# Two attention layers on one core: hand-ordered first and last steps, paired loads, and a second bank for two late outs

## The reference

```python
# layer 0 (layer 1 alike, with its own mask: k = -inf and v = 0 where masked)
xn = layernorm(x) * ln_w + ln_b
q = xn @ Wq + bq
k = xn @ Wk + bk + (1.0 - src_mask) * -1e6
q = softmax(q over the features of a head)
k = softmax(k over the tokens)
v = (xn @ Wv + bv) * src_mask
att = einsum('bnhd,bnhl->bhdl', k, v)
y = einsum('bnhd,bhdl->bnhl', q, att)
scale, shift = split(silu(emb) @ W_emb + b_emb)
h = layernorm(y) * ln2_w + ln2_b
h = h * (1 + scale) + shift
x = x + silu(h) @ W_out + b_out
```

## Time and profile before

| | us |
|---|---|
| median of 3 runs | 306.34 |
| lowest and highest | 303.88 and 311.64 |
| the profiled execution's own time | 306.14 |
| its span, first to last instruction | 304.4 |
| mean granted TensorE clock | 0.947 of full |

### The profile page before, as it was taken

How to read it: one execution, slowest core, us unless ns; L and a number is a source line. 1 busy time by engine, 2 the same in 40 slices (tenths; PEclk the granted TensorE clock), 3 DMA queues, 4 the chain that set the end, 5 groups by cost and what they waited for, 6 DMA issues and landing times.

```text
span 304.4 us, 8956 instructions
## 1 busy us (share of the span) xinstructions
PE 264.1 (87%) x2746; PEld 191.2 (63%) x2746; DVE 261.3 (86%) x870; ACT 215.9 (71%) x497; POOL 222.6 (73%) x296
## 2 busy tenths in 40 slices
PE   1615899779999999998999999999989999987564
PEld 1302576556777777775777677777767776765342
DVE  2791677899999999999999999999998888789851
ACT  1352776678887888877899989999997987663210
POOL 1342336799999999999999989999998776753300
PEclk9955999999999999999999999999999999999755
DMA  7599956874566676796469866565599779753945
GB/s 230 181 264 277 266 66 189 158 100 103 107 100 128 131 148 122 122 129 124 104 99 120 151 92 133 129 123 126 128 137 132 155 147 156 165 132 106 163 103 182
DMA packets 91006, 43.59 MB, mean 143 GB/s; under 512 B 71952, under 2 KB 85072, under 8 KB 90960
## 3 DMA queue, kind: packets, MB, share of 16 engines
q1 hardware_dynamic: 84048, 34.90, 62.5%
q10 hardware_dynamic: 6912, 8.13, 9.2%
HBM read 21.94 MB, written 4.29 MB: 86 GB/s over the span
## 4 chain that ended last, share of the span: by engine, by line
PE 50%; POOL 21%; issue 14%; DMA 6%; DVE 4%; ACT 2%; SPq 1%; ACTq 1%; POOLq 0%; DVEq 0%
PE ps_qv L1262 16%; PE ps_eo L1299 11%; PE ps_k L1242 9%; PE ps_y L1361 5%; POOL h L217 5%; POOL y_z L642 4%; POOL h_half L212 4%; POOL k_mask L630 4%; DMA zt_hi<-z_hi 3%; PE ps_eo L1280 3%; PE ps_eq L1333 2%; PE ps_eq L1314 2%; DMA m1c<-in_mask_col 2%; DMA film_ab<-film_rows 1%; POOL x_rstd L608 1%
## 5 line engine op out<-in xcount | busy, mean ns | idle before, releaser
L478 ACT ACTIVATE v<-ps_qv,v_mask 128x256 f32<-128x256 f32 x64 | 30.2, 472 | 41.8 <-PE ps_qv L1262 41.8
L1262 PE MATMUL ps_qv<-w_hi,zt_hi 128*128 128x512 f16 x128 | 48.7, 381 | 1.7 <-DVE q_sub L920 1.7
L1262 PE MATMUL ps_qv<-w_lo,zt_hi 128*128 128x512 f16 x128 | 48.5, 379 | 0.0
L1262 PE MATMUL ps_qv<-w_hi,zt_lo 128*128 128x512 f16 x128 | 48.5, 379 | 0.0
L642 POOL TENSOR_SCALAR y_z<-y_n,y_rstd,y_shift 128x256 f32<-128x256 f32 x64 | 37.3, 592 | 10.8 <-DVE y_shift L1015 10.8
L1299 PE MATMUL ps_eo<-wo_hi,gt_hi 128*128 128x256 f16 x128 | 37.3, 291 | 7.5 <-DVE x_all L1055 7.5
L1242 PE MATMUL ps_k<-zt_hi,w_hi 128*128 128x256 f16 x128 | 35.4, 276 | 8.3 <-issue 8.3
L673 POOL TENSOR_TENSOR x_all<-x_all,row_b 128x512 f32<-128x512 f32 x32 | 41.0, 1280 | 0.0
L1299 PE MATMUL ps_eo<-wo_hi,gt_lo 128*128 128x256 f16 x128 | 37.2, 291 | 0.0
L1299 PE MATMUL ps_eo<-wo_lo,gt_hi 128*128 128x256 f16 x128 | 37.2, 291 | 0.0
L1361 PEld LDWEIGHTS ps_y<-att_e,eq_t 128*128 128x128 f32 x256 | 33.8, 190 | 5.1 <-issue 1.0
(11 more groups left out here) (98 smaller groups left out, 682.1 us busy)
## 6 DMA issues: line engine op xcount, KB each, us to landing
film_ab<-film_rows SPq DMA_DIRECT2D x32, 256.0 KB, 3.8
m_row<-mask_rows SPq DMA_DIRECT2D x32, 128.0 KB, 3.4
out<-x_all SPq DMA_DIRECT2D x16, 256.0 KB, 2.5
x_all<-in_x ACTq DMA_DIRECT2D x2, 1024.0 KB, 10.8
wemb<-in_w_emb ACTq DMA_DIRECT2D x2, 1024.0 KB, 7.7
x_all<-in_x ACTq DMA_DIRECT2D x1, 1536.0 KB, 13.5
w_raw<-in_w_in SPq DMA_DIRECT2D x1, 768.0 KB, 4.9
w_raw<-in_w_in ACTq DMA_DIRECT2D x1, 768.0 KB, 13.8
```

The costliest lines, as they stand in the source:

```text
L478: nc.scalar.activation(part(v[p], t), ps_qv[:, t * BANK + D:(t + 1) * BANK], ACT.Copy, scale=v_mask[a.layer][:, m:m + 1]).then_inc(v_ready ...
L1262: last = mm(part(ps_qv, t, BANK), zz[p][:, (t * C + c) * P:(t * C + c + 1) * P], w[l][:, c * W + D:(c + 1) * W], start=(n == 0), stop=(n = ...
```

## The change

Every engine gets functions first_steps() and last_steps() beside step(s). The first and last items are called one by one with at(j), in an order of their own, and only the items between go through the loop. The step in the loop has another order too, with small offsets (item(s, 0) to item(s, 18)).

Loads: x comes in pairs of sequences (X_GROUPS: 1, 1 and then seven times 2), the first pair after z_high(0) and no longer before ACT's loop. wemb, wo, w_raw[1] and row_b[1] are issued one at a time at later steps, and wo and wemb have a semaphore each. w_raw[0] is loaded in two parts, k columns and qv columns, after the two small mask rows. What is loaded is the same.

film_scale stays on POOL up to item 29 (SCALE_ON_DVE = 30), film_shift up to item 27 as before. The out products of items 29 and 31 (ASIDE) go to ps_k, which is free after the last k_shift; items 30 and 31 so don't wait for the residual just before them. late_products is defined, and nothing calls it. UNUSED stays 0.

The core of the diff (the lists of first_steps are cut, and the weights' and film operations that hang on a value of s are moved with the rest):

```diff
-    FILM_ON_DVE = LAST - 4
+    SCALE_ON_DVE, SHIFT_ON_DVE = LAST - 2, LAST - 4
+    ASIDE = (LAST - 3, LAST - 1)
+    X_GROUPS = ((0, 1), (1, 1)) + tuple((i, 2) for i in range(2, B, 2))
+        def out_bank(a):
+            return ps_k[:, :] if a.index in ASIDE else ps_eo[:, :]
# SP
             load(col[:, :], columns, col_in)
-            load(w_raw[0][:, :].rearrange("p (c n) -> p c n", c=C), w_in[0].rearrange("(c p) n -> p c n", p=P), w_in_s[0])
             load(m0r[:, :], mask0_row, mask_in)
             load(m1r[:, :], mask1_row, mask_in)
+            load_columns(0, D, wk_in[0])
+            load_columns(D, 2 * D, wqv_in[0])
             def step(s):
...
+                do(film_rows_of, item(s, 10))
+                do(mask_row, item(s, 7))
+                do(store, item(s, 18))
+                do(turn_g_high, item(s, 13))
+                do(turn_g_low, item(s, 13))
+                do(turn_z_high, item(s, 6))
+                do(turn_z_low, item(s, 6))
# ACT
-            load_sequences(2, 4, x_in[2])
                 if s == 0:
-                    load_chunked(wo_raw[0], w_out[0], C, w_late_in[0])
-                    load_chunked(wemb[0], w_emb[0], EC, w_late_in[0])
-                    load_sequences(6, 4, x_in[3])
+                    load_group(2)
                 if s == 1:
-                    load_chunked(w_raw[1], w_in[1], C, w_in_s[1])
-                    load(row_b[1][:, :], rows[1].partition_broadcast(P), rows_in[1])
-                if s == 2:
-                    load_sequences(10, B - 10, x_in[4])
+                    load_chunked(wemb[0], w_emb[0], EC, wemb_in[0])
+                if s == 2:
+                    load_group(3)
+                    load_chunked(wo_raw[0], w_out[0], C, wo_in[0])
+                if s == 3:
+                    load_chunked(w_raw[1], w_in[1], C, wqv_in[1])
+                if s == 4:
+                    load_group(4)
+                    load(row_b[1][:, :], rows[1].partition_broadcast(P), rows_in[1])
+                if 5 <= s < len(X_GROUPS):
+                    load_group(s)
# POOL
+            def step(s):
+                do(k_scaled_heads, item(s, 4))
+                do(x_power, item(s, 1))
+                do(y_power, item(s, 6))
+                do(normalise_y, item(s, 6))
+                do(film_shift, item(s, 7))
+                do(add_out_bias, item(s, 1))
+                do(film_scale, item(s, 6))
+                do(x_variance, item(s, 0))
# DVE
+            def first_steps():
+                fold_columns(0)
+                fold_columns(1)
+                x_statistics(at(0))
+                x_aggregate(at(0))
+                mask_rows()
+                block_masks()
+                x_offset(at(0))
+                x_statistics(at(1))
...
+                z_low(at(0))
+                silu_cond()
+                sum_of_parts()
+                k_weights(0)
+                x_statistics(at(2))
+                k_weights_low(0)
...
+                k_shift(at(0))
+                qv_weights_low(0)
+                value_masks()
+                x_statistics(at(4))
+                x_statistics(at(5))
+                z_low(at(2))
+                q_maximum(at(0))
...
+            def step(s):
+                do(att_scale, item(s, 5))
+                do(y_variance, item(s, 6))
+                do(gate, item(s, 8))
+                do(q_maximum, item(s, 4))
+                do(y_offset, item(s, 6))
+                do(x_offset, item(s, 1))
+                do(residual, item(s, 10))
+                do(q_shift, item(s, 4))
+                do(g_low, item(s, 8))
+                do(k_shift, item(s, 3))
+                do(y_sums, item(s, 5))
+                do(x_statistics, item(s, 0))
+                do(y_divide, item(s, 5))
+                do(x_aggregate, item(s, 0))
+                do(y_statistics, item(s, 5))
+                do(k_sums, item(s, 3))
+                do(y_aggregate, item(s, 5))
+                do(z_low, item(s, 1))
+            def last_steps():
...
+                gate(at(30))
+                film_scale(at(31))
+                g_low(at(30))
+                film_shift(at(31))
+                residual(at(28))
+                gate(at(31))
+                residual(at(29))
+                g_low(at(31))
+                residual(at(30))
+                residual(at(31))
# PE
+            def first_steps():
+                k_weight_rows(0)
+                qv_weight_rows(0)
+                project_k(at(0))
+                unused_products()
+                film_products(0)
+                project_qv(at(0), 0)
+                project_qv(at(0), 1)
+                film_part_sums(0)
+                turn_exp_k(at(0), at(-1))
+                project_k(at(1))
...
+            def step(s):
+                do(project_k, item(s, 3))
+                do(attention_out, item(s, 5))
+                do(turn_exp_k, item(s, 4), item(s, 10))
+                do(project_qv, item(s, 3), 0)
+                do(attend, item(s, 4), item(s, 5))
+                do(project_qv, item(s, 3), 1)
+                do(project_out, item(s, 9), item(s, 4))
+                do(turn_exp_q, item(s, 4), item(s, 4))
+            def last_steps():
...
+                attention_out(at(31))
+                project_out(at(26), at(-1))
+                project_out(at(27), at(-1))
+                project_out(at(28), at(-1))
+                project_out_aside(at(29))
+                project_out(at(30), at(-1))
+                project_out_aside(at(31))
```

596 lines of the change are left out of this document (417 added, 179 removed).

## The result

The changed kernel takes 293.7 us (median of 4 runs, 292.72 to 294.65); the kernel before took 307.68 beside it (303.88 to 311.64). The ratio is 0.9626, with a 95% interval of 0.954 to 0.9711. Executions more than 1.5% above the fastest of their kernel are left out of a ratio but not of a median, so a ratio isn't the quotient of the two medians. The forecast was 294.0. The profiled execution took 292.72 us for a span of 290.9.

What follows compares the result with a forecast made beforehand. No engine alone was the bound: PE, DVE and POOL are full together in layer 0, with idle time at the ends. Start 28.0, middle 230.0 and end 34.1 sum to 292.1, plus 1.7 around the span: 294 us, range 285 to 305.

Steps and rivals of the forecast that it cites:

- The start: Span up to project_k(1): forecast 28.0 us against 34.05, bounds 25 and 32, a gain of 6.0.
- It runs at the half clock as it does now: project_k(0) on PE, starting at 17: half clock, 2.7 us, ending at 19.7.
- The middle: From project_k(1) to project_k(31): forecast 230.0 us against 229.96, no gain, bounds 226 and 239.
- I give that 2 us of the 3.5: z transposes issued together and earlier: 2 us less of PE's 3.5 us idle time from 140 to 265 us.
- 0.2 x 15 = 3.0: Layer 0, POOL waiting for DVE's y_offset between y_power and normalise_y: 0.2 us in 15 steps, 3.0 us more.
- PE's work between the two project_k is nearly the same: Middle, project_k(1) to project_k(31): nearly the same set of products as before, 222 us of PE work.
- The end: From project_k(31) to the end: forecast 34.1 us against 40.4, bounds 31.5 and 38.
- With items 29 and 31 in ps_k, out(31) waits only for its own transpose ... Gain 2.4: End, g_low(31) to finish: no wait for the residual before out(31), 9.4 or 9.5 us against 11.9.
- Ahead of it DVE is full and its order decides: End, before g_low(31): film_scale to POOL 1.2 us, film_ab wait 1.1, other DVE idle time 1.6 gone.
- (b): Rival: start lost, x pairs arrive one by one behind weights, project_k(1) at 32 to 33, time 299; chance 0.12.
- (c): Rival: POOL's layer 0 wait is 0.8 us, not 0.2, 9 us more, 303; chance 0.10.
- (d): Rival: every step grows by a DVE wait at g_low or q_shift; 0.75 us each gives 315; chance 0.06.

Runs made afterwards that it cites:

- e6: The changed kernel with UNUSED = 6, six unused products between project_k(0) and the film products: 292.77 us, ratio 0.9551.
- e1: The changed kernel with the five large x loads and old bunching of weight loads: 300.13 us, ratio 0.9802.
- e5: The changed kernel with k_scaled_heads moved between y_power and normalise_y on GpSimd: 292.82 us, ratio 0.9603.
- e4: The changed kernel with film_scale of items 28 and 29 back on DVE: 295.25 us, ratio 0.9629.
- e3: The changed kernel with ASIDE empty, all out products in ps_eo again: 294.11 us, ratio 0.9656.
- e12: The kernel before with unused products ahead of the out products of items 28 to 31: 306.39 us, ratio 0.9881.
- e11: The changed kernel with item 31's statistics of y moved back behind film_shift(30) and g_low(29): 296.53 us, ratio 0.9687.
- e2: The kernel before, in its old order, with x in pairs and late weight loads one at a time: 312.89 us, ratio 1.0215.
- e8: The changed kernel with SP's transpose of the low part of z issued one call later: 328.60 us beside 308.0 for the kernel before.

## Why the prediction was right, and where by luck

The time, 293.7 for 294.0, is closer than the working deserves. The three cuts are within 1.5 us each (0.8 under, 1.1 over, 1.5 under the forecast), but terms within each were wrong and partly cancelled.

**The start (27.18 for 28.0).** Right: the order of the causes, film products at 20.99 for 21, y_power(0) at 38.08 for 41, transposes under 6 us. Wrong: "I take 4 to 5 us for zt_lo(0)" (2.9), the first x load (x_statistics(0) at 4.20, not 5.5), and "It runs at the half clock as it does now": PE had idled only 2.80 us before project_k(0), not 3.36 after a wait of 8.62 and a short burst as in the earlier trace rows, and the clock was full. All of this 2.6 us ended in the wait of 5.13 us for wemb, so it moved project_k(1) by little. The bound of project_k(1) is wemb, as the text had it. From the film products to project_k(1) PE doesn't idle and takes 6.2 us for 6.7, as project_qv(0) took 3.0 and not 3.5. "x_statistics(4) ... until 27.8" was wrong: it started at 24.28, and DVE doesn't hold project_k(1). It comes next, though (0.36 us in e6).

By the estimate from the Trainium skill's rule on batching (DMA: Bandwidth & Descriptors, "Bandwidth") the small loads would have cost 2 us. Pairs of 512 KB land in 4.7 us and the 1024 KB of wemb in 7.8, so a megabyte in two loads strictly one behind the other would be dearer, 9.4 (an estimate from these two). e1, with large loads, is nevertheless the slower by 6 us, because what they hold up is the transposes. The price of a load here is what it puts in front of others. The Trainium skill's rule on the clock (TensorE: Matmul & The Clock Gate, "Loop structure matters more than you think") holds for the film products, which ran at the lower level behind the wait for wemb (1.94 us, 1.07 in e6); of project_qv(0), which I feared whole at half clock by that rule, only the first three products were slow (0.61, 0.63 and 0.43 us, then 0.38).

**The middle (231.14 for 230.0).** The two terms were mis-sized in opposite ways. "I give that 2 us of the 3.5" to the transposes: it was 3.1 before project_k, and the wait of project_qv for q_shift fell too (1.7 to 0.2 us in the same view). "0.2 x 15 = 3.0" for POOL's handover: the wait is 0.30 in 14 of layer 0's items and the step 7.76 for 7.70, much as forecast, but e5 shows it worth 0.9 to 1.3, since PE's layer 1 products lie under it. What I didn't count is that "PE's work between the two project_k is nearly the same": it is 2.4 us more (225.0 against 222.6 busy), chiefly the out products of one more item (25 groups against 24 in that view), 1.42 us, and its attend. The new order has project_out one item closer behind project_k. That isn't a loss: the same work is missing from the end. PE's idle time between the cuts fell from 7.4 to 6.1 us only, and 6.0 of what is left lies in layer 0.

**The end (32.58 for 34.1).** 9.15 us from g_low(31) for 9.5, and no wait for film_ab. film_scale: 1.2 forecast, 1.1 in e4. The step that failed is "With items 29 and 31 in ps_k, out(31) waits only for its own transpose ... Gain 2.4": the second bank is worth 0.2 at most (e3). From g_low(31) to the end the changed kernel did gain 2.8: out(31) starts 2.0 us sooner behind g_low(31) (3.88 for 5.84) and takes 0.8 less (1.94 for 2.73, where I had "kept" the half clock). But with one bank out(31) starts only 0.2 us later after k(31) (e3), and e12 shows the old order gaining 3.0 by the clock alone (4.03 to the start, 1.48 for the product). What made out(31) late before is that the outs ahead of it ran at half clock, each followed by a residual. I had read the residual as the wait because the chain in the earlier trace rows names it; it was between two products, each twice too long. And "Ahead of it DVE is full and its order decides" was said but priced at 1.6 of idle time; the order of item 31's statistics is worth 2.5 (e11). Some of the end's gain is also only moved ahead of the cut at k(31): DVE works 24.9 us behind it and not 27.5, of which film_scale explains 1.2. These parts aren't additive: e11's late item also finds PE colder (0.977 of full over the run against 0.987).

**The rivals.** (b), the start lost to pairs arriving late, is what e2 shows, but only in the old order: DVE waits 10.1 us there and 3.7 in the changed kernel (1.20 and 2.46). (c), a wait of 0.8, didn't come in layer 0. (d), a per-step wait, didn't come, but e8 shows that a misplaced transpose makes just that, about 1.1 us on each of 30 steps. So (d) was near in the order of SP, not in DVE's, where I had looked.

What stays open: why e8's loop settles at this size; what lets the transposes ahead of k(4) land late in some executions and not in others; and whether the small gains of e5 and e6 exist, which the spread of the runs (some 2 to 4 us) hides.

## What to carry to other kernels

Price an order and the loads that feed it together: here the order alone gave half of the gain, and the loads alone a loss. When a chain of waits alternates a product and an eviction, look at the clock of the products before adding a bank, since at full speed the wait may be elsewhere. In a drain the last item goes first on the shared engine; and where two engines are both full, removing a wait on one buys only what the other leaves.
